# The small experts of layer 3: two experts' rows held in the array's column halves while their weights stream past, a pipeline one pair deep, later first loads, and one test for the unused groups

## The reference, cut to what matters

```python
xb = x[token_buf].reshape(E, CAP, H)                       # rows of each expert, at most CAP = 192
gu = jnp.einsum('ech,ehf->ecf', xb, W_gate_up)             # 192 -> 2 x 464
g, u = jnp.split(gu, 2, axis=-1)
inter = jax.nn.silu(g) * u
yb = jnp.einsum('eci,eih->ech', inter, W_down)             # 464 -> 192
yb = yb * w_buf.reshape(E, CAP, 1)
routed = jnp.zeros((T, H), x.dtype).at[token_buf].add(yb.reshape(E * CAP, H))
shared = jax.nn.silu(x @ Wsg) * (x @ Wsu) @ Wsd            # a dense expert that sees every token
return (routed + shared).reshape(B, S, H)
```

## Time and profile before

| | us |
|---|---|
| median of 3 runs | 874.93 |
| lowest, highest run | 866.03, 877.20 |
| profiled execution | 877.28 |
| its span (first to last instruction) | 875.2 |
| TensorE busy in it | 780.3 (89%) |
| mean granted TensorE clock | 0.913 |
| `Many` loop, first to last product | 475.6 to 580.4 |
| `Few` loop, first to last product | 583.0 to 634.5 |

### The profile page before, as it was taken

One profiled execution on the slowest core, in us unless ns is written; L12 is line 12 of the kernel. 1 busy time (PEld: TensorE's weight loads), 2 busy tenths in 40 slices (PEclk: granted clock), 3 DMA queues, 4 the chain that ended last, 5 costly groups with the idle time before them and its releaser, 6 DMA issues. The chain is left out here.

```text
span 875.2 us, 16547 instructions
## 1 busy us (share of the span) xinstructions
PE 780.3 (89%) x5587; PEld 594.9 (68%) x5587; DVE 379.2 (43%) x1115; ACT 304.3 (35%) x721; POOL 271.9 (31%) x314
## 2 busy tenths in 40 slices
PE   8997999798999988999978989989978968889885
PEld 5775897466585658999646868877836557756663
DVE  1444222224263257788593212211115298545443
ACT  2530222223464147665411212211123454425440
POOL 0004455000002116775024534432201043135771
PEclk9987999787989999999999999988689978969996
DMA  9814899300000052230133977757682240541224
GB/s 361 306 28 158 292 307 258 95 1 1 1 2 1 0 208 73 63 84 1 34 110 122 381 268 220 214 174 235 224 227 60 95 120 2 214 129 36 75 68 104
DMA packets 41490, 117.10 MB, mean 134 GB/s; under 512 B 5856, under 2 KB 12976, under 8 KB 40912
## 3 DMA queue, kind: packets, MB, share of 16 engines
q1 hardware_dynamic: 33888, 97.20, 33.0%
q0 software_dynamic: 7536, 19.06, 8.1%
HBM read 104.53 MB, written 11.70 MB: 133 GB/s over the span
## 5 line engine op out<-in xcount | busy, mean ns | idle before, releaser
L1694 ACT ACTIVATE L_hid<-bank 116x384 f32<-116x384 f32 (+1 forms) x38 | 17.6, 462 | 92.9 <-PE bank L1745 58.5
L1430 POOL TENSOR_TENSOR ssm_w_low<-ssm_wbc,ssm_w_high 128x512 fp32r<-128x512 f32 x24 | 31.1, 1299 | 38.5 <-ACT ssm_w_high L1385 38.5
L156 ACT ACT_TABLE_LOAD x19 | 24.4, 1283 | 52.0 <-PEq L161 51.8
L1999 POOL TENSOR_TENSOR L_s_up<-L_s_hid,L_s_up 116x288 f32<-116x288 f32 (+1 forms) x10 | 8.3, 828 | 107.5 <-ACT L_s_up L1993 107.5
L1812 DVE TENSOR_TENSOR L_act_many<-L_hid,bank 116x384 f32<-116x384 f32 x28 | 15.5, 554 | 58.4 <-ACT L_hid L1694 58.4
L1968 PE MATMUL bank<-xn,par_L1f 128*116 128x288 f32 (+1 forms) x128 | 32.5, 472 | 6.4 <-issue 6.4
L1345 PE MATMUL bank<-ssm_x_high,ssm_w_high 128*128 128x288 f32 x96 | 33.8, 352 | 3.8 <-DVE bank L1473 2.3
L1440 POOL TENSOR_TENSOR ssm_grown<-ssm_less,xn 128x576 f32<-128x576 f32 x23 | 32.9, 1430 | 7.9 <-ACT ssm_less L1413 5.3
L1669 POOL DMA_INDIRECT y_rows_L<-L_many_y,L_many_rows_out x21 | 20.7, 985 | 46.2 <-ACT L_many_y L1712 38.1
L1479 DVE TENSOR_TENSOR_SCAN ssm_state<-ssm_decay,bank 128x576 f32<-128x576 f32 x24 | 32.5, 1354 | 0.8
L1645 POOL DMA_INDIRECT L_many_xr<-x_rows_L,L_many_rows_in x27 | 26.8, 994 | 11.9 <-POOL L_many_rows_in L1658 5.7
(11 more groups left out here) (544 smaller groups left out, 2006.8 us busy)
## 6 DMA issues: line engine op xcount, KB each, us to landing
L_w<-in_L2w SPq DMA_DIRECT2D x18, 696.0 KB, 5.4
L_more<-in_L2w SPq DMA_DIRECT2D x14, 696.0 KB, 6.3
L_w<-in_L0w SPq DMA_DIRECT2D x12, 576.0 KB, 4.9
L_w<-in_L2w SPq DMA_DIRECT2D x18, 384.0 KB, 6.5
ssm_wbc<-in_wBC SPq DMA_DIRECT2D x24, 256.0 KB, 2.7
L_w<-in_L3w SPq DMA_DIRECT2D x5, 1152.0 KB, 12.4
L_more<-in_L2w SPq DMA_DIRECT2D x14, 384.0 KB, 7.7
L_more<-in_L0w SPq DMA_DIRECT2D x9, 576.0 KB, 4.2
```

The lines of the kernel that those rows point to most:

```text
L156: self.nc.scalar.activation(self.unread[:, at:at + 1], self.p["ones"][:, 0:1], func)
L1430: pool.tensor_tensor(w_low[t % NW][:, :], wbc[t % NW][:, :], w_high[t % NW][:, :], ALU.subtract).then_inc(low, 1)
L1694: act.activation(self.X.hid[part][:, 0:at], self.X.up_bank[2 * part][0:self.X.N, 0:at], ACT.Silu).then_inc(self.acted, 1)
```

## The change

In `Few`: `upwards` holds the rows (64 columns for each of the two experts, in the two column halves) and streams 464 columns of weights past them: 4 products over 128 features and 4 over 64, in place of 32. What comes out has rows on partitions, so the SiLU and the product run once over 128 x 464, and four transposes and a copy by ScalarE (`turn_hidden`, `hid_turned`, `hid_in`) bring it into the layout of `act_few`. The loop is a pipeline: step `q` turns the hidden values of pair `q`, makes the up products of pair `q + 1`, turns the rows of pair `q + 2` and makes the down products of pair `q`. `w1` and `w2` count on two semaphores, in both loops. The loads for pairs that are not in use are left out (`comes`). The first loads of `Few` are issued inside `Many`'s loop, behind its second step. The first group of steps stands by itself, and one test skips all the others. The index table is one column wider (169), and the counts in the plan are at least 3.

```diff
-MANY_UNITS, FEW_UNITS = 3 * (MANY_STEPS + 2), FEW_STEPS + 2
+MANY_UNITS, FEW_UNITS = 3 * (MANY_STEPS + 2), FEW_STEPS + 3
+LEAST = 3
@@ Pairs
     def steps_in_use(self, eng, n, body):
-        with eng.Fori(0, self.GROUPS) as g:
-            with eng.If(g * (2 * SETS * GROUP) < n):
-                with eng.Fori(0, GROUP) as i:
-                    for h in range(SETS):
...
+        def group(g):
+            with eng.Fori(0, GROUP) as i:
+                r = i + g * GROUP
+                q = r * SETS
+                with eng.If(q * 2 < n):
+                    body(r, q, 0)
+                    with eng.If((q + 1) * 2 < n):
+                        body(r, q + 1, 1)
+
+        group(0)
+        with eng.If(n > 2 * SETS * GROUP):
+            with eng.Fori(1, self.GROUPS) as g:
+                with eng.If(g * (2 * SETS * GROUP) < n):
+                    group(g)
+    def comes(self, eng, n, q):
+        return eng.If(q * 2 < n)
@@ Pairs.sp
+            with self.comes(sp, n, q + 2):
...
+            if after and h == 1:
+                with sp.If(r < 1):
+                    after.load(sp, 0)
+                    after.load(sp, 1)
@@ Pairs.pool
+            to = h if U > 1 else 1 - h
+            pool.wait_ge(self.gates_in, q + self.ROWS_AHEAD - 1)
+            pool.wait_ge(self.turned, (q + (self.ROWS_AHEAD - 1)) * U)
...
@@ Many.pe
-            pe.wait_ge(self.loaded[2 * h], r * 32 + 32)
+            pe.wait_ge(self.loaded[2 * h], r * 16 + 16)
...
+            pe.wait_ge(self.loaded_second[2 * h], r * 16 + 16)
             self.downwards(pe, q, h, 0)
@@ Few
+    def upwards(self, pe, h):
+        X, I = self.X, self.X.I
+        banks = X.up_bank[2 * h:2 * h + 2]
+        for a in range(2):
+            for j, rows in enumerate(self.ROWS):
+                pe.matmul(banks[a][rows, 0:I], self.xt[h][:, 0, rows], self.w1[2 * h + j][:, I * a:I * a + I], start=True, stop=False)
+        for a, made in ((0, self.gate), (1, self.up)):
+            half = slice(64 * a, 64 * a + 64)
+            for j, rows in enumerate(self.ROWS):
+                mm = pe.matmul(banks[a][rows, 0:I], self.xt[h][half, 1, rows], self.w1[2 * h + j][half, 2 * I:3 * I], start=False, stop=True)
+            mm.then_inc(made, 1)
+    def turn_hidden(self, pe, q, h):
+        X, N = self.X, self.X.N
+        pe.wait_ge(self.hidden, q + 1)
+        for f in range(X.C):
+            mm = pe.transpose(X.hid_bank[0:N, R * f:R * f + R], X.hid[h][:, N * f:N * f + N], self.T.p["ident"])
+        mm.then_inc(self.hid_turned, 1)
@@ Few.pe
         def step(r, q, h):
+            self.turn_hidden(pe, q, h)
+            with self.comes(pe, n, q + 1):
+                pe.wait_ge(self.xt_in, q + 2)
+                for j in range(2):
+                    pe.wait_ge(self.loaded[2 * (1 - h) + j], r * 16 + (32 if h else 16))
+                self.upwards(pe, 1 - h)
+            pe.wait_ge(self.xt_in, q + 2)
+            self.turn(pe, h, 0, r + 2)
+            self.downwards(pe, q, r, h)
@@ Few.act
+            act.wait_ge(self.hid_turned, q + 1)
+            act.copy(self.X.act_few[:, :, :], cols(self.X.hid_bank[0:self.X.N, 0:self.X.C * R], self.X.C)).then_inc(self.hid_in, 1)
+            e = self.experts_of(act, (q + 2) * 2 + self.place)
+            with self.comes(act, n, q + 1):
+                act.wait_ge(self.gate, q + 2)
+                act.activation(self.X.hid[1 - h][:, :], self.X.up_bank[2 * (1 - h)][:, 0:self.X.I], ACT.Silu).then_inc(self.acted, 1)
             self.weigh(act, r, q, h, 0)
+            act.wait_ge(self.y_in, q + (self.AT_FIRST + 1))
+            self.take_gates(act, e, h, r + 2)
@@ route
-            dve.tensor_copy(X.plan[0:1, P:P + 2], T.bank[2][0:1, 4:6]).then_inc(plan_known, 1)
+            dve.tensor_scalar(X.plan[0:1, P:P + 2], T.bank[2][0:1, 4:6], float(LEAST), None, ALU.max).then_inc(plan_known, 1)
@@ run_pairs, sync
             many.load(sp, 1)
-            few.load(sp, 0)
-            few.load(sp, 1)
-            steps = [(loop, loop.sp(sp)) for loop in (many, few)]
+            steps = [(many, many.sp(sp, few)), (few, few.sp(sp))]
```

More of the change, by code:

```diff
@@ L1824 @@
     GROUPS = FEW_GROUPS
[L1825 removed]
+    GATES, LAST_UP, LAST_DOWN, AT_FIRST, ROWS_AHEAD = 1, (1, 1), (1, 1), 2, 3
     OWNERS = [[(slice(0, FEW), 0), (slice(FEW, R), 1)]]
[L1828 to L1846 removed]
@@ L1848, in downwards @@
[L1848 to L1852 removed]
+    ROWS = slice(0, FEW), slice(FEW, R)
+    def upwards(self, pe, h):
[9 more added lines that the diff above has]
+            mm.then_inc(made, 1)
@@ L1853, in downwards @@
         for f in range(X.C):
-            if f % 2 == 0:
-                pe.wait_ge(self.hidden, q * 2 + (f // 2 + 1))
-            for j in range(2):
-                rows = slice(FEW * j, FEW * j + FEW)
+            for j, rows in enumerate(self.ROWS):
                 mm = pe.matmul(bank[rows, 0:DIM], X.act_few[:, f, rows], self.w2[2 * h + j][0:X.N, DIM * f:DIM * f + DIM],
@@ L1874, in act @@
+        self.turn(pe, 0, 0, 1)
+        pe.wait_ge(self.xt_in, 1)
+        for j in range(2):
+            pe.wait_ge(self.loaded[j], 16)
+        self.turn(pe, 1, 0, 1)
+        self.upwards(pe, 0)
+        self.steps_in_use(pe, n, step)
     def act(self, act):
+        n = self.in_use(act)
         def step(r, q, h):
-            self.silu(act, q, 0, 0)
-            e = self.experts_of(act, (q + 1) * 2 + self.place)
-            self.silu(act, q, 1, 1)
-            act.wait_ge(self.y_in, q * self.UNITS + self.AT_FIRST)
@@ L1898, in dve @@
-        self.steps_in_use(dve, self.in_use(dve), step)
+            with self.comes(dve, n, q + 1):
+                dve.wait_ge(self.acted, q + 2)
+                dve.wait_ge(self.up, q + 2)
+                self.product(dve, 1 - h)
+            self.take_next(dve, q + 2, h)
+        self.take_next(dve, 0, 0)
+        self.take_next(dve, 1, 1)
+        dve.wait_ge(self.acted, 1)
+        dve.wait_ge(self.up, 1)
+        self.product(dve, 0)
+        self.steps_in_use(dve, n, step)
 class Resident:
@@ L2689, in _ @@
             few.gather(pool, 1, 0)
-            steps = [(loop, loop.pool(pool)) for loop in (many, few)]
+            steps = [(many, many.pool(pool))]
+            pool.wait_ge(few.gates_in, 1)
+            pool.wait_ge(few.turned, 1)
+            pool.tensor_copy(few.rows_in[0][:, :], X.idx[:, MANY_UNITS + 2:MANY_UNITS + 3, 0]).then_inc(few.idx_in, 1)
+            pool.wait_ge(few.idx_in, 3)
+            few.gather(pool, 0, 0)
+            steps.append((few, few.pool(pool)))
             for loop, n in steps:
```

134 lines of the change are left out of this document (55 added, 79 removed).

## The result

The kernel after takes 847.1 us (4 runs, 841.5 to 851.5) against 876.1 for the kernel before beside it: a ratio of 0.971, interval 0.966 to 0.976. It is faster by over 2%, and the time lies in the predicted range, 7 us under the 854 forecast. Every kernel here, the one before too, runs some per cent slower in some of its executions: medians are over all runs, ratios over the fast ones alone.

What follows compares the result with a forecast made beforehand. `Many` was taken as bound by TensorE's products, the stretches around it by waits and low clock. Terms 5.2 + 1.2 + 11.5 - 1.0 + 4.4 = 21.3 off 877.28 gave 856.0, for a median 854; range 842 to 864.

Steps and rivals of the forecast that it cites:

- the gap ahead of the tail: Between `Few`'s last product and the tail: seven group tests become one, 2.0 of 6.38 us stay, 4.4 gone; bounds 2 and 6.
- Later first loads in `Many`: In `Many`: `Few`'s eight loads leave the queue ahead of the third pair, removing its wait and slow records, 5.2 us.
- Rival (b): In `Many`: the wait comes back at the fifth pair, giving back up to 5.2 us, 859; chance 0.08.
- From `Many` to `Few`: Gap of 2.60 us between the loops: three group tests become one, 1.2 us gone; bounds nothing and 2.2.
- rival (c): Skip in both loops: one jump over a copied group body costs what the tests cost, 859 to 860; chance 0.09.
- The up products: In `Few`: sixteen records of 464 columns per pair, neighbours in different column halves overlapping by two, take 4.15 us, against 5.5.
- Rival (a): In `Few`: column halves don't overlap at 464 columns, `Few` 48.4 us, 862; 873 if held-row loads aren't hidden; chance 0.10.
- `Few`'s waits: In `Few`: waits of 1.5 and 2.3 us for the fourth and fifth pairs' `w1`; `Few` 40 us, 11.5 gone.
- The clock: Low clock after idle stretches in the new chain of `Few` adds 1.0 us in all; bounds 0 and 3.
- Rival (e): In `Few`: waits for DMA before each pair keep the clock at 0.50 throughout, 886, slower; chance 0.07.
- The table's width: In the routing: `at_block` 169 wide, 36 instructions on the stage's path, costs nothing.
- rival (d): In the routing: odd, unaligned tables cost 145 ns more each, 5.2 us in all, 859; chance 0.04.

## Why the prediction was right, and where it was not

**The whole.** The sum for the stage was 21.3 us; its three profiles of the kernel after give 23.8, 23.5 and 22.1 (198.92 less 175.16, 175.42 and 176.84). Single terms were off in both directions, and most of that cancelled, which is luck: against the forecast `Few` gave 5.2 us more, the gap ahead of the tail 1.9, the tail 1.4 and the first turn 0.5, while `Many` gave 3.9 less and the gap between the loops went 2.6 the wrong way.

**Later first loads in `Many`: right.** 5.2 predicted, 5.5 in the kernel that has this without the new `Few`, and no wait at the third or the fifth pair. That the place of the loads is the cause is shown by putting them back. Rival (b), a wait at the fifth pair, did not come. That the size fits so well owes to the profile: the 5.2 were read from the very execution that the 5.5 are measured against, and with the smaller waits of other executions the same loads are worth 1.9 to 2.6.

**From `Many` to `Few`: wrong sign.** Predicted -1.2, bounds 0 and -2.2; measured +1.4. I counted tests and did not price a jump. The bounds left a loss out without a reason, although rival (c) had the mechanism: one jump over a copied body costs what the tests cost. Behind `Many` it costs more (3.6 us, where all of the gap was 2.6). Behind `Few` rival (c) was wrong, and so was the forecast's 2.0 us that stay: 0.07 stay. Both treated the two jumps as one thing, and they differ by the code between, if not in proportion to it.

**The up products: mis-sized, 4.15 for 2.65 us.** The record in one half was right (0.394 against 0.40). The eight of the first plane were put at (4 + 1) x 0.394 = 1.97 and take 1.71 with the change of shape in it, so they overlap by two with nothing left over. The eight of the second plane were put at 1.97 too, as overlapping by two; they take 0.94, since they differ in column halves and in feature halves and overlap by four. The row for that was there: the earlier trace rows has `Many`'s second plane, which overlaps by features alone, at little over half of its first (0.84 us for 1.49, start to start). With the test of `comes` hidden (0.45 predicted), the warm step is 0.58 + 2.65 + 0.37 + 1.45 = 5.05 us, which the kernel with small loads and the one with four sets both show, not 7.1. Rival (a), no overlap, is excluded: the kernel that puts all up products into one half is what it describes, and its `Few` takes 618.7 - 572.0 = 46.7 us from the first up product, where the rival had 48.4 without any overlap. By the Trainium skill, "TensorE: Matmul & The Clock Gate", Part 3, a weight load hides behind a running product only in another row group; the two column halves use the same one, and 1.71 us for eight records with eight loads of 0.13 us leaves no room for loads in series. Here the measurement decides.

**`Few`'s waits: the transfers were right, the work was not.** The prediction had `w1` of the fourth pair landing 21.4 us after the first up product and TensorE ready at 19.9. TensorE's wait for it ended at 591.93 - 571.13 = 20.8, and it was ready at 588.21, which is 17.1. The wait is 3.72 for 1.5 (5.11 and 5.28 in the other two profiles) because the products are faster than I thought. The fifth pair's was then there in time: the second 9 us between landings were too long, it took at most 6.7 (591.93 to 598.63), with a later start for everything behind the long wait. In sum: without waits and at full clock `Few` takes 28.7 us (the kernel with four sets, loops to the count), and my sum had 36.2. Of the 7.5 us by which I was too high, 2.6 went back into waits and the slow clock behind them (4.3 + 3.1 us in the profile of after, for 3.8 + 1.0). `Few` came out at 35.9, 39.2 and 38.8 for 40 or 41; 37 to 43 were predicted, so the first lies just below. The forecast's step that failed is that hardly any work would be saved: it was about 10 us of busy time at full speed, and the waits took part of it back.

**The clock.** 1.0 us predicted. Behind `Many` the first up products take 3.36 for 1.78, behind the long wait 3.28: 3.1 us, the upper bound of 3; in the other two profiles, with longer waits, the slow records add up to 4.4 to 4.7. With no gap (1.11 us instead of 4) and no wait, it is nothing. Rival (e), `Few` at the low clock throughout, did not come: 0.90.

**The tail.** I left 0 for its cold start ("up to 1.5 could come back"): 1.4 in one profile of after, 0.2 and 0.8 in the others.

**The table's width.** 0 predicted; 0.1 measured; rival (d), with 145 ns each, is excluded by 4 ns. The unaligned slices that the Trainium skill, "VectorE: DVE Perf Modes", section "Mode 2×_1P — pack two bf16 into one 32-bit read", would slow down show no such price here.

**The median.** 854 for 847.1. 2.5 us of that is the stage. The rest lies in the kernels' scatter: the profiled execution that the sum started from had 8 us of low clock in layers that the change leaves alone, and taking only its 2.35 us above the median off did not undo that. The ratios of the three comparisons, 0.967 to 0.977, include the 0.976 predicted.

## What to carry to other kernels

When a stage turns from work to transfers as its bound, a further gain ahead of it can be waited away, and the next edit has to be the transfers' start: three us of gap removed brought 0.5 alone, and removed gaps counted once the buffers of the loop before were used to load two pairs more. Count a skip by the branch that it adds, not only by the tests that it saves: over a small body it took 0.2 us here, over larger ones 3.3 to 5.5, not in proportion to their size. So read it from the trace, and let a loop run to its count where that is possible. And where products differ in column halves as well as in feature halves, expect an overlap of nearly four before you cost them (0.94 us here, where an exact quarter is 0.8).

## What the runs showed that I had not expected

- One taken branch of TensorE over a large body takes 3.3 to 4.1 us behind `Many`, 5.5 over the old body of `Few`, 3.5 over four bodies of the new one and 0.215 over two. Instruction fetches are on the way meanwhile. Where between two and four bodies the step lies, no run shows, and why `Many`'s larger body costs less than the old `Few`'s is open.
- Products in 64-column halves: eight records of 464 columns take 3.23 us in one half, 1.71 in two, and over 64 features 1.71 and 0.94. The order A, B, A, B or A, A, B, B makes no difference with two records each; eight in a row cost 2.22 us for 1.52.
- ScalarE and VectorE standing still for over 5 us together in `Many`'s first step in one execution, and `Many` 2.3 to 2.5 us longer in three others. What does it stayed open.
